# A later lag for turned chunks, another order of the scores, and a block transpose in two parts

## The reference

```python
q = (text_hidden @ Wq).reshape(B, T_text, N_HEADS, HEAD_DIM).transpose(0, 2, 1, 3)
...
scores = jnp.einsum('bhtd,bhsd->bhts', q, k) / scale
...
attn = jax.nn.softmax(scores, axis=-1)
...
out = jnp.einsum('bhts,bhsd->bhtd', attn, v)
out = out.transpose(0, 2, 1, 3).reshape(B, T_text, N_HEADS * HEAD_DIM)
return out @ Wo
```

## Time and profile before

| | |
|---|---|
| time, median of 3 runs | 1785.72 us (1777.26 to 1786.11) |
| time of the profiled execution | 1788.69 us |
| its span, first to last instruction | 1786.8 us |
| TensorE busy in the span | 1678.9 us (94%) |
| VectorE, ScalarE, GpSimd busy | 1245.4, 1031.2 and 665.0 us |
| mean granted TensorE clock | 0.981 of 2.4 GHz |

### The profile page before, as it was taken

The page is one execution under the profiler, slowest core; times in us unless marked ns, Lnnn a source line. Parts: engine busy times, 40 slices in busy tenths (PEclk is TensorE's granted clock), DMA queues, the critical chain, the costliest instruction groups (busy, mean ns, idle before and its releaser), DMA issues.

```text
span 1786.8 us, 28843 instructions
## 1 busy us (share of the span) xinstructions
PE 1678.9 (94%) x9650; PEld 1494.5 (84%) x9650; DVE 1245.4 (70%) x3410; ACT 1031.2 (58%) x2101; POOL 665.0 (37%) x417
## 2 busy tenths in 40 slices
PE   7999698999999999999999999999999999999996
PEld 7998687878888888988888888788888888888985
DVE  5645476777777778777777777777777676847547
ACT  4444265566666666666556666566666566644542
POOL 1210423343344444433333333343333444164535
PEclk9999898999999999999999999999999999999999
DMA  5234532434343433434243434343434342531433
GB/s 190 93 121 146 187 90 64 90 78 92 80 84 84 84 82 79 92 76 102 62 83 88 111 73 96 75 91 80 87 76 86 79 84 50 113 99 46 121 91 100
DMA packets 127438, 165.52 MB, mean 93 GB/s; under 512 B 45214, under 2 KB 106304, under 8 KB 127168
## 3 DMA queue, kind: packets, MB, share of 16 engines
q1 hardware_dynamic: 85360, 140.67, 31.0%
q10 hardware_dynamic: 38912, 14.80, 4.5%
q0 software_dynamic: 3024, 8.26, 1.7%
HBM read 113.62 MB, written 24.89 MB: 78 GB/s over the span
## 4 chain that ended last, share of the span: by engine, by line
PE 48%; DMA 15%; SPq 12%; DVE 11%; ACT 6%; issue 6%; POOL 1%; ACTq 1%; POOLq 0%; DVEq 0%
SPq L799 12%; DMA rden_store<-b_rden 10%; PE b_turn L870 6%; PE b_out L899 5%; PE b_out L889 4%; PE a_bank L347 4%; PE b_out L890 4%; PE b_out L891 4%; PE b_score L856 4%; PE b_score L858 4%; PE b_score L857 4%; DMA b_keyed<-b_by_block 3%; ACT b_pT_hi L943 2%; ACT b_p L949 2%; DVE b_by_block L1051 2%
## 5 line engine op out<-in xcount | busy, mean ns | idle before, releaser
L1056 DVE TENSOR_TENSOR b_pT_lo<-b_turn,b_pT_hi 125x512 fp32r<-125x512 f32 (+1 forms) x768 | 477.0, 622 | 333.4 <-ACT b_pT_hi L943 331.1
L943 ACT CAST b_pT_hi<-b_turn 125x512 fp32r<-125x512 f32 (+1 forms) x768 | 408.1, 532 | 255.0 <-PE b_turn L870 242.5
L1031 DVE CUSTOM_DVE_ANT_0 b_p<-b_score,b_mask_add 128x500 f32<-128x500 f32 x672 | 449.0, 668 | 30.2 <-PE b_score L858 18.7
L889 PE MATMUL b_out<-b_pT_hi,b_c_hi 125*128 125x512 f32 (+1 forms) x768 | 351.4, 458 | 74.1 <-DVE b_pT_lo L1056 73.4
L870 PEld LDWEIGHTS b_turn<-ident,b_p 128*125 128x125 f32 x2304 | 372.3, 188 | 56.7
L870 PE MATMUL b_turn<-ident,b_p 128*125 128x128 f32 x2304 | 379.8, 274 | 0.0
L949 ACT ACTIVATE b_p<-b_p,b_shift 128x1500 f32<-128x1500 f32 x224 | 347.7, 1552 | 47.8 <-DMA rden_store<-b_rden 45.7
L1197 POOL TENSOR_TENSOR b_oT_over<-b_oT,b_oT_hi 128x896 fp32r<-128x896 f32 x32 | 67.7, 2115 | 586.9 <-ACT b_oT_hi L973 549.6
L890 PE MATMUL b_out<-b_pT_lo,b_c_hi 125*128 125x512 f32 (+1 forms) x768 | 284.3, 370 | 0.0
L891 PE MATMUL b_out<-b_pT_hi,b_c_raw_over 125*128 125x512 f32 (+1 forms) x768 | 283.9, 370 | 0.0
L856 PE MATMUL b_score<-b_cT_hi,b_q_hi 128*128 128x500 f32 x672 | 265.3, 395 | 0.3 <-DVE b_cT_lo L1142 0.3
(11 more groups left out here) (253 smaller groups left out, 2584.3 us busy)
## 6 DMA issues: line engine op xcount, KB each, us to landing
b_keyed<-b_by_block SPq DMA_DIRECT2D x512, 48.0 KB
cT_in<-in_ctxT SPq DMA_DIRECT2D x32, 750.0 KB, 6.8
b_c_raw<-in_ctx SPq DMA_DIRECT2D x32, 750.0 KB
q_store<-a_fold_in_or_q_stage SPq DMA_DIRECT2D x16, 896.0 KB, 4.2
q_in<-q_store SPq DMA_DIRECT2D x32, 448.0 KB, 3.8
b_rden_all<-rden_store ACTq DMA_DIRECT2D x32, 256.0 KB, 3.5
b_rden_all<-rden_store ACTq DMA_DIRECT2D x32, 192.0 KB, 3.8
b_mask_in<-in_mask SPq DMA_DIRECT2D x32, 187.5 KB, 5.1
```

Of the source, the lines that this page charges most:

```text
L889: pe.matmul(out, hi, pT_hi[:, n % 3, 0:w], start=(c == 0), stop=False)
L943: act.copy(pT_hi[:, n % 3, 0:w], turn_bank[n % 3][0:CK, 0:w]).then_inc(hi_done, 1)
L1031: dve.tensor_tensor_reduce(out=p[slot % 2][:, u, keys], in0=score_bank[j][:, 0:FW], in1=mask_add[:, b, keys], scale=1.0, scalar=-3.0e38, o ...
L1056: dve.tensor_tensor(pT_lo[:, n % 3, 0:w], turn_bank[n % 3][0:CK, 0:w], pT_hi[:, n % 3, 0:w].bitcast(F32), ALU.subtract).then_inc(lo_done, 1)
```

## The change

Turning and weighing lag two steps more, and so do the load of the reciprocals, `scale_out`, the rounding of oT, the projection and the norm. Reciprocals and their store stay. In odd slots the scores come in another order, so that the third third of unit 0 is filled at step 4 instead of 2; the last third of unit 1 stays at step 6 and that of unit 2 at step 10. The block transpose becomes two instructions of six chunks each, at steps 5 and 6, and the moves wait for both.

```diff
-        TURN_LAG = CH + 3
+        TURN_LAG = CH + 5
         PV_LAG = TURN_LAG + 2
 
 
-        RDEN_AT, STORE_AT, LOAD_AT = 3, 4, 11
-        SCALE_AT, ROUND_AT = 4, 5
+        RDEN_AT, STORE_AT, LOAD_AT = 3, 4, 1
+        SCALE_AT, ROUND_AT = 6, 7
         LATE_SLOTS, LOAD_LATE, SCALE_LATE = range(2), 2, 3
-        PROJECT_AT, NORM_AT, NORM_OUT_AT = CH + 10, CH + 11, 2 * CH + 8
-        BLOCKS_AT = 5
+        PROJECT_AT, NORM_AT, NORM_OUT_AT = CH + 12, CH + 13, 2 * CH + 10
+        BLOCKS_AT = (5, 6)
+        BLOCK_PARTS = len(BLOCKS_AT)
...
+        def fill_of(slot, m):
+
+
+            if slot % 2 == 0:
+                return m // FILLS, m % FILLS
+            return ((0, 0), (0, 1), (1, 0), (0, 2), (1, 1), (1, 2), (2, 0), (2, 1), (2, 2))[m]
+
+        def last_fill(slot, u):
+            return max(m for m in range(FILLS * units(slot)) if fill_of(slot, m)[0] == u)
...
-                sp.wait_ge(blocks_turned, n + 1)
+                sp.wait_ge(blocks_turned, BLOCK_PARTS * (n + 1))
...
-                if at := slot_due(i, n, 1, LOAD_AT, first, last, LOAD_LATE):
+                if at := slot_due(i, n, 2, LOAD_AT, first, last, LOAD_LATE):
                     load_rden(*at)
...
-            def turn_blocks(i, slot):
+            def turn_blocks(i, slot, part):
 
 
                 n = 2 * i + slot // 2
-                dve.wait_ge(exp_done, PUNITS * i + unit0[slot] + 1)
-                if n:
-                    dve.wait_ge(keyed_loaded, MOVES * n)
-                own = p[0][:, 0, :]
-                keys = bass.AP(own.tensor, own.offset, [own.ap[0], [32, QUADS], [CK, CH], [1, 32]])
-                dve.transpose(by_block[:], keys).then_inc(blocks_turned, 1)
+                if part == 0:
+                    dve.wait_ge(exp_done, PUNITS * i + unit0[slot] + 1)
+                    if n:
+                        dve.wait_ge(keyed_loaded, MOVES * n)
+                count = CH // BLOCK_PARTS
+                own = p[0][:, 0, part * count * CK:]
+                keys = bass.AP(own.tensor, own.offset, [own.ap[0], [32, QUADS], [CK, count], [1, 32]])
+                dve.transpose(by_block[:, :, part * count:(part + 1) * count, :], keys).then_inc(blocks_turned, 1)
...
-                    if n // CH % 2 == 0 and n % CH == BLOCKS_AT:
-                        turn_blocks(i, n // CH)
+                    if n // CH % 2 == 0 and n % CH in BLOCKS_AT:
+                        turn_blocks(i, n // CH, BLOCKS_AT.index(n % CH))
```

More of the change, by code:

```diff
@@ L844, in fill @@
             def fill(i, slot, m, first):
-                u, j, b = m // FILLS, m % FILLS, slot // 2
+                (u, j), b = fill_of(slot, m), slot // 2
                 n = FILLS * unit0[slot] + m
@@ L852, in fill @@
                     pe.wait_ge(fill_taken, PFILLS * i + n - FILLS + 1)
-                out = score_bank[j][:, 0:FW]
+                out = score_bank[m % FILLS][:, 0:FW]
                 keys = slice(j * FW, (j + 1) * FW)
@@ L978, in exp_step @@
                     for slot, m in fills_at(at[1]):
-                        if m % FILLS == FILLS - 1:
-                            exps(at[0], slot, m // FILLS)
+                        u, j = fill_of(slot, m)
+                        if j == FILLS - 1:
+                            exps(at[0], slot, u)
             def lag_step(i, n, first, last=False):
@@ L1030, in scores @@
                 keys = slice(j * FW, (j + 1) * FW)
-                dve.tensor_tensor_reduce(out=p[slot % 2][:, u, keys], in0=score_bank[j][:, 0:FW],
+                dve.tensor_tensor_reduce(out=p[slot % 2][:, u, keys], in0=score_bank[m % FILLS][:, 0:FW],
                                          in1=mask_add[:, b, keys], scale=1.0, scalar=-3.0e38,
@@ L1036, in shifts @@
             def shifts(i, slot, u):
-                dve.wait_ge(fill_taken, PFILLS * i + FILLS * (unit0[slot] + u + 1))
+                dve.wait_ge(fill_taken, PFILLS * i + FILLS * unit0[slot] + last_fill(slot, u) + 1)
                 dve.tensor_scalar(top_min[:], top[:, slot % 2, u, :], -float(X_SCALE), None, ALU.mult, ALU.min,
                                   accum_out=shift[:, slot % 2, u:u + 1]).then_inc(shift_done, 1)
-            def turn_blocks(i, slot):
+            def turn_blocks(i, slot, part):
                 n = 2 * i + slot // 2
-                dve.wait_ge(exp_done, PUNITS * i + unit0[slot] + 1)
-                if n:
-                    dve.wait_ge(keyed_loaded, MOVES * n)
-                own = p[0][:, 0, :]
-                keys = bass.AP(own.tensor, own.offset, [own.ap[0], [32, QUADS], [CK, CH], [1, 32]])
-                dve.transpose(by_block[:], keys).then_inc(blocks_turned, 1)
+                if part == 0:
[6 more added lines that the diff above has]
+                dve.transpose(by_block[:, :, part * count:(part + 1) * count, :], keys).then_inc(blocks_turned, 1)
             def p_rest(i, n):
@@ L1106, in fill_step @@
                     scores(i, slot, m, first)
-                    if m % FILLS == FILLS - 1:
-                        shifts(i, slot, m // FILLS)
+                    u, j = fill_of(slot, m)
+                    if j == FILLS - 1:
+                        shifts(i, slot, u)
             def lag_step(i, n, first, last=False):
```

## The result

The changed kernel is slower: 1885.46 us median of four runs (1877.09 to 1890.13) against 1782.38, now of four as well (1777.26 to 1786.11), a ratio of 1.0575 with a 95% interval of 1.0525 to 1.0625. 1747 us had been forecast.

What follows compares the result with a forecast made beforehand. TensorE was taken as the bound, its waits as what can be won: -36.8 - 13 - 39.2 + 5 + 44 + 1.5 = -38.5 us from the profiled 1788.7 gives 1750, set against the median as 1747 us; range 1711 to 1782.

Steps and rivals of the forecast that it cites:

- Removing A: Step 2 of a pair: loading the reciprocals two steps later ends the wait for their store; -36.8 us and -13 of clock.
- Removing B: Steps 17 to 19 and 41 to 43: awaiting the moved blocks two steps later ends TensorE's stalls there; -39.2 us.
- +5 for the few moves late by over 1.8 us: Waits for moved blocks: what stays of those stalls where moves exceed the net gain of 1.8 us; bounds 0 and 20.
- A: TensorE's stall at step 2 of a pair, behind the slow store of the reciprocals; 36.8 us, plus 13 of clock.
- The pile: ScalarE's work between a slot's first and fourth chunk delays weighing at steps 22 and 46; 1.5 us per three-unit slot, +44 us.
- The order of scores: Three-unit slots: with the lag, the new order puts extra work on ScalarE; included in the +44 us.
- The two parts: Block transpose at steps 5 and 6: the second instruction hides behind TensorE's steps; nothing on the path, 3 us if uncovered.
- The tail: End of the kernel: the first y2 load waits for the last copy, two steps later; +1.5 us, bounds 0 and 2.1.
- SyncE's queue: The second element's moves stand behind a context load that waits for GpSimd; nothing, bounds 0 and 20 us.
- The third: Rival at step 5 of three-unit slots: moves land late despite two steps; 1804 us at 2 us mean lateness, chance 0.07.
- gaps at steps 19 and 43 behind the block copy: Sign in TensorE's weighing that would show the moves are late.
- The fourth: Rival at the store: block moves and mask loads delay it as much, so its stall stays; 1797 us, chance 0.04.

Runs made afterwards that it cites:

- e3: The kernel before with only the load of the reciprocals two steps later; 1752.52 us (ratio 0.9905).
- e1: The changed kernel with the store of the reciprocals at step 5 instead of 4, behind the wait for the moves; 1756.53 us (0.9927).
- e6: The changed kernel with the same store in 128 pieces of 16 or 12 bytes instead of 512 or 384 of 4; 1747.07 us (0.9894).
- e10: The kernel before with the reciprocals transposed on VectorE and stored as rows in four DMAs of 128-byte pieces, nothing else; 1717.24 us (0.9715).
- e12: The changed kernel with the reciprocals transposed on VectorE and stored as rows in four DMAs, nothing else; 1748.06 us (0.9814).
- e4: e1 with the rounding of oT at step 8 instead of 7; 1734.22 us (0.9813).
- e7: e4 with the scores of the three-unit slots back in their old order, unit by unit; 1761.91 us (0.998).
- e2: The changed kernel with the block transposition in one piece at step 5; 1864.13 us (1.0511).
- e8: e4 with the block transposition in one piece at step 5; 1730.03 us (0.9793).
- e5: The changed kernel with the reciprocals and their store one step earlier; 1930.45 us (1.0904).
- e11: e8 with the reciprocals transposed on VectorE and stored as rows in four DMAs, the store at step 4; 1714.28 us (0.9704).

## Why the prediction was wrong, point by point

**Removing A** was right: 36.8 us and the clock, 14.9 measured against 13, are gone, and e3 shows that the load's place alone does it. That the load of values lengthens a store beside it holds too. By the semaphore events, the 2 KB stores of before, nearly all issued 0.6 to 3.3 us behind that load, land after 13.3 us (median of 32). Those of e1, issued ahead of it (1045.79 against 1047.48), land after 9.6, a case that the prediction had no run of. What the reading left out is that the store slows the load as well, and that most of the store's own time comes of its pieces (e6). In e10 the store is short and the load of the reciprocals stands in its old place. The values are issued at 1028.27, as by chance before, and GpSimd goes on at 1039.13 instead of 1042.38:

```profile
1028.27 0.28 SPq L790 DMA_DIRECT2D b_c_raw<-in_ctx  x1
```

```profile
1039.13 1.50 POOL L1170 TENSOR_SCALAR b_c_hi<-b_c_raw 125x1536 fp32r<-125x1536 f32 x1 [4.03 <-DMA b_c_raw<-in_ctx]
```

The 2 KB stores of e10 land after 6.7 us (median of 32), inside the 10.4 us that the prediction counted up to the wait, and the wait goes.

**Removing B** is the step that failed, with its "+5 for the few moves late by over 1.8 us (bounds 0 and 20)". It weighed only when the moves start against when their blocks are wanted. It didn't ask what ScalarE issues between the old place of that wait and the new one. That was the store, which in "Removing A" merely "stays at step 4"; by moving the wait from step 39 to 41 the change let it out ahead. The price was 115 us at step 43 and 27 of clock. The second half was caught and not the first, since its moves are issued later: in the pair shown the issuing for the first half ends 0.7 us before the store (1032.29 + 10.69 against 1043.68), for the second 2.7 us after it (1078.59 + 12.06 against 1087.98):

```profile
1032.29 10.69 SPq L810 DMA_DIRECT2D b_keyed<-b_by_block  x16
```

```profile
1043.68 0.40 ACTq L967 DMA_DIRECT2D rden_store<-b_rden  x1
```

The rest of this step held: with the store behind the wait (e1) the stalls for the moves are down to some 2 us, of 41 before. Even so e1 gains 0.7% where 2.2% had been forecast for the change; how much of A that chip had to give is not shown.

**The pile** was right: 1.5 us forecast, 1.49 measured in e1 and 1.50 in e12, with the rounding at its head (e4) and the gap of 0.85 shown at step 22. That the sum agrees to a hundredth is partly luck: 1.3 had been forecast at step 22 and 0.2 at 23, and 1.1 and 0.15 were measured, with 0.24 at step 20 that the working didn't have. In the changed kernel only the first half shows it; in the second, step 46 shows 2.8 us in all, where e1 has 16.6 once the stall at step 43 is gone.

**The order of scores** is in the sum by its cost, the pile, and not at nothing, as e7's expectation has it; e7 adds that the old order under the later lag would have cost 1.8 us a half. **The two parts** at nothing hold (e2, e8). **The tail** at 1.5 us (bounds 0 and 2.1) was too small: the longest wait of y2's turning for its load is 1.2 us before and 5.2 in the changed kernel; with the short store of e12 it is 1.9.

**SyncE's queue** at nothing (bounds 0 and 20) doesn't hold in the changed kernel. In most pairs the moves start within 0.1 us of the transposition's end, in the pair shown 2.1 us behind it, after the context load at 1078.16. But the issues of the second half's moves, 9.4 to 10.6 us from the first to the last before, take 11.0 to 14.7 us in 14 of the 15 pairs; the pair with 9.7 loses 0.2 us at step 43. So that lateness probably brings the second half under the store; no run changes it alone. By itself it costs nothing: with the short store (e6), or the store behind the wait (e1), the issues take 9.4 to 11.2 us again and no such stall comes of them. What makes the queue late is not shown.

**The rivals.** The third, late moves, had the sign and the place, "gaps at steps 19 and 43 behind the block copy", and 0.07. Its price was a mean of 2 us in all halves; it was 8 to 11 in one of two, from another cause, with a fall of the clock that the rival left out. The fourth supposed that the store is delayed by the moves. The store took 10.4 us in the changed kernel (median of the 32 of 2 KB) and 9.6 in e1; it was the moves that waited.

The runs show that the store decides, by its place (e1, e5) and its pieces (e6). Not shown apart is whether the moves' data lay in place while their counts were held, or was itself held up. The trace's DMA packets go only part of the way. The last data packet of the moves shown is recorded as ended at 1091.7, and their last count came 6.4 us later, where it is 0.3 us in most first halves of this trace. But the store's own 512 pieces are recorded as ended by 1089.4, 5.6 us before its first count, so such a record doesn't tell that data has landed. And the mask load behind the moves was held as data: its packets of 1500 bytes that started between 1092 and 1093 took 6.6 us each (median of 10), those after 1099 some 0.2. The Trainium skill (DMA: Bandwidth & Descriptors, "Queues, rings and completion order") says that a semaphore increment lands only after every earlier write of its DMA engine, across its queues. The trace agrees: 5.7 us without one count of the moves, until the store's came.

## What to carry to other kernels

When a wait is moved later on an engine, list what that engine issues between the two places: all of it now runs ahead of the wait, its DMAs beside the transfers that are awaited. Price a store of a few KB by its pieces and not by its bytes alone; here 512 of 4 bytes took 9.6 us and held up a neighbour's transfers, and turning them into rows first made the kernel before 2.8% faster, more than any rearrangement around them. A pile of work on one engine can be worked out to 0.1 us from its rows, so when such a sum misses by 100 us, look for a term that isn't in it.

## What was not expected of the hardware

A 2 KB store on one queue stopped the counts of sixteen 48 KB moves on another for 5.7 us, and the DMA engines moved 4 to 10 GB/s meanwhile. That a last dimension which isn't contiguous is lowered to one descriptor per element is in the Trainium skill (DMA: Bandwidth & Descriptors, "Rules for kernel authors"). The trace agrees: e6 has 20,480 packets fewer, which is 32 x 384 + 32 x 256. The runs add the price. With the reciprocals stored as rows, the load of values went faster as well: it landed after 14.1 us before and 8.1 in e11 (medians by the semaphore events), and GpSimd's wait for it was 227.2 us before, 86.7 in e10 and 27.0 in e11.
